# Grouped attention layer: where the query and value evacuations stand in the softmax rounds

## The reference, cut to what matters

```python
q = hidden_state @ Wq + bq
k = encoder_hidden_state @ Wk + bk
v = encoder_hidden_state @ Wv + bv
q = q.reshape(b, l, KVH, GROUPS, HD).transpose(0, 2, 3, 1, 4)
...
scores = jnp.einsum('bkgld,bksd->bkgls', q, k) * scale
scores = scores + encoder_attention_mask[:, :, None, :, :]
attn = jax.nn.softmax(scores, axis=-1)
out = jnp.einsum('bkgls,bksd->bkgld', attn, v)
out = out.transpose(0, 3, 1, 2, 4).reshape(b, l, H)
out = out @ Wo + bo
x = out + hidden_state
...
return (x - mu) * jax.lax.rsqrt(var + EPS) * gamma + beta
```

## Time and profile before

| what | value |
|---|---|
| median of 3 runs | 2687.87 us (2686.5 to 2689.95) |
| profiled execution | 2687.89 us, its span 2686.1 us |
| busy, share of the span | PE 2477.0 us, 92%; DVE 1280.0 us, 48%; ACT 1089.2 us, 41%; POOL 1106.1 us, 41% |
| chain that ended last | PE 79%, DVE 8%, ACT 6%, POOL 3%, issue 3% |
| grouped layer | about 810 to 1200 us of the span |

### The profile page before, as it was taken

One profiled execution on the slowest core, in us unless ns is written; L12 is line 12 of the kernel. 1 busy time (PEld: TensorE's weight loads), 2 busy tenths in 40 slices (PEclk: granted clock), 3 DMA queues, 4 the chain that ended last, 5 costly groups with the idle time before them and its releaser, 6 DMA issues.

```text
span 2686.1 us, 47930 instructions
## 1 busy us (share of the span) xinstructions
PE 2477.0 (92%) x18464; PEld 2080.4 (77%) x18464; DVE 1280.0 (48%) x2527; ACT 1089.2 (41%) x3705; POOL 1106.1 (41%) x1972
## 2 busy tenths in 40 slices
PE   7999998999997788758889899999899999899999
PEld 5887886888886666647778788888788888688887
DVE  4555564323226878764555533322355555432322
ACT  4555553111117777754565511111355555311111
POOL 2454446400035888873454571003335444640000
PEclk9999999999998989878999999999999999999999
DMA  4112213111122222221232241102211211311100
GB/s 154 56 56 74 86 48 95 59 47 48 57 71 72 82 91 70 74 67 45 94 111 77 82 129 48 47 23 69 87 48 49 84 53 48 95 59 48 47 32 16
DMA packets 110320, 181.25 MB, mean 67 GB/s; under 512 B 7888, under 2 KB 43408, under 8 KB 109072
## 3 DMA queue, kind: packets, MB, share of 16 engines
q1 hardware_dynamic: 110096, 178.19, 20.2%
HBM read 132.02 MB, written 46.14 MB: 66 GB/s over the span
## 4 chain that ended last, share of the span: by engine, by line
PE 79%; DVE 8%; ACT 6%; POOL 3%; issue 3%; DMA 1%; SPq 0%; DVEq 0%; POOLq 0%; ACTq 0%
PE banks L317 70%; PE banks L453 4%; ACT plain_high L697 4%; PE banks L480 3%; DVE neg_max L948 2%; DVE plain_high L944 2%; POOL plain_high L1268 1%; DVE plain_work L953 1%; PE banks L504 1%; DVE rounded_work L1046 1%; DVE rounded_work L1020 1%; DVE stats L1072 1%; POOL rounded_high L308 0%; PE banks L442 0%; ACT plain_high L684 0%
## 5 line engine op out<-in xcount | busy, mean ns | idle before, releaser
L317 PE MATMUL banks<-rounded_work,rounded_low 128*128 128x512 f32 (+1 forms) x2688 | 534.7, 357 | 58.4 <-issue 35.2
L1268 POOL TENSOR_SCALAR plain_high<-plain_high,inv_sum 128x128 f32<-128x128 f32 (+1 forms) x1024 | 389.6, 403 | 410.2 <-DVE inv_sum L966 409.7
L317 PEld LDWEIGHTS banks<-rounded_work,rounded_low 128*128 128x128 f32 x2688 | 446.7, 200 | 125.6 <-issue 53.7
L317 PE MATMUL banks<-rounded_work,rounded_high 128*128 128x512 f32 (+1 forms) x2400 | 485.4, 356 | 8.4 <-DMA rounded_work<-ctx_split 5.8
L925 ACT ACTIVATE plain_work<-banks,columns 128x512 f32<-128x512 f32 x192 | 132.5, 690 | 865.3 <-PE banks L317 865.3
L317 PEld LDWEIGHTS banks<-rounded_work,rounded_high 128*128 128x128 f32 x2400 | 397.1, 191 | 75.8 <-issue 10.0
L1244 DVE CAST rounded_work<-plain_work 128x512 fp32r<-128x512 f32 x192 | 99.3, 517 | 694.1 <-ACT plain_work L925 682.9
L317 PE MATMUL banks<-rounded_low,rounded_work 128*128 128x512 f32 x1728 | 413.1, 391 | 0.0
L317 PE MATMUL banks<-rounded_high,rounded_work 128*128 128x512 f32 (+1 forms) x1728 | 392.7, 380 | 0.0
L317 PEld LDWEIGHTS banks<-rounded_low,rounded_work 128*128 128x128 f32 x1728 | 322.3, 188 | 68.8 <-issue 3.0
L317 PEld LDWEIGHTS banks<-rounded_high,rounded_work 128*128 128x128 f32 x1728 | 311.8, 190 | 60.4 <-issue 1.4
(11 more groups left out here) (101 smaller groups left out, 3055.3 us busy)
## 6 DMA issues: line engine op xcount, KB each, us to landing
plain_work<-x SPq DMA_DIRECT2D x96, 256.0 KB, 2.8
plain_work<-mlp_w SPq DMA_DIRECT2D x96, 256.0 KB, 2.7
rounded_work<-ctx_split SPq DMA_DIRECT2D x24, 1024.0 KB, 5.9
u<-plain_work SPq DMA_DIRECT2D x48, 256.0 KB, 3.1
plain_work<-u SPq DMA_DIRECT2D x12, 1024.0 KB, 7.2
x<-plain_work SPq DMA_DIRECT2D x48, 256.0 KB, 2.1
plain_work<-attention_w SPq DMA_DIRECT2D x44, 256.0 KB, 2.7
plain_work<-inputs_t SPq DMA_DIRECT2D x8, 1024.0 KB, 8.0
```

What stands on the lines that cost most here:

```text
L317: mm = pe.matmul(dst, lhs(i), rhs(j), start=first and n == 0, stop=last and n == 2, skip_group_check=True)
L1268: last = pool.tensor_scalar(part, part, inv_sum[:, R % 2, r, g:g + 1], 1.0, ALU.mult, ALU.mult)
```

## The change

In act_gqa the evacuation of the next pair's first queries moves from behind round 2's last exponential to between those of banks 1 and 2, and the evacuation of the next pair's values moves likewise in round 3. In dve_gqa the low part of the queries moves from behind the inversions and dve_again to ahead of the inversions. Counts and shapes of the instructions are the same, and PE, POOL and SP have the same order as before.

```diff
@@ act_gqa
                 act_heads(act, y, p, 0)
                 if more:
                     act_keys(act, y, p + 1, 0)
-                act_round(act, y, p, 2, (p, 1), nothing)
-                if more:
-                    act_queries(act, y, p + 1, 0)
+
+                def queries():
+                    if more:
+                        act_queries(act, y, p + 1, 0)
+
+                def values():
+                    if more:
+                        act_values(act, y, p + 1, 0)
+
+                act_round(act, y, p, 2, (p, 1), queries)
                 act_heads(act, y, p, 1)
-                act_round(act, y, p, 3, (p, 2), nothing)
-                if more:
-                    act_values(act, y, p + 1, 0)
+                act_round(act, y, p, 3, (p, 2), values)
                 act_heads(act, y, p, 2)
@@ dve_gqa
                 if more:
                     dve_keys(dve, y, p + 1, 0)
-                dve_round(dve, y, p, 2, (p, 1), nothing)
+
+                def queries():
+                    if more:
+                        dve_queries(dve, y, p + 1, 0)
+
+                dve_round(dve, y, p, 2, (p, 1), queries)
                 if p:
                     dve_again(dve, y, 2 * p - 1)
-                if more:
-                    dve_queries(dve, y, p + 1, 0)
                 dve_heads(dve, y, p, 1)
```

## The result

| | kernel before | changed kernel |
|---|---|---|
| median (range, runs) | 2687.49 us (2684.92 to 2689.95, 12) | 2695.91 us (2692.7 to 2703.1, 12) |
| ratio, 95% interval | 1 | 1.0035 (1.0027 to 1.0044) |
| profiled execution, its span | 2687.89 us, 2686.1 us | 2694.08 us, 2692.3 us |

A forecast was written before the change was run, and what follows sets the result against it. No engine is full; a pair is a ring of waits between engines. First pair 1.97, two pairs 0.85 each, four 0.07 each and slow value blocks 4.98 sum to 8.93 us on 2687.87: 2696.8 us, range 2694 to 2700.

The forecast's parts named there:

- Queries on ScalarE and VectorE, -0.07 us: Round 2: second inversion 0.71 us later, but the queries' low part (0.78 us) no longer behind it; net -0.07 us.
- GpSimd, +0.78: Round 2: the low part delays the first inversion, so GpSimd's normalisation starts and ends 0.78 us later.
- The values' end, and the wait on ScalarE: Round 3, fifth pair: value matmuls end at 1041.21; ScalarE, there at 1040.47, waits with eight exponentials queued behind.
- 0.7 us and more in each of seven pairs: Sign: ScalarE's idle ahead of line 744, ended by the value matmuls, is at least this long in every pair.
- above 3 us where the block is slow: Sign: that same ScalarE idle exceeds 3 us where the value matmuls run at 1.2 GHz.
- Pair lengths: Round 2 to next round 0: about 21.2 us, or 23.7 with a slow value block, instead of 20.33 and 21.11.
- VectorE's wait for ScalarE's heads: Sign: VectorE's wait at L993, L998 in the changed program, grows.
- no wait for TensorE ahead of the mask addition: Sign: VectorE's wait for TensorE ahead of the next mask addition is gone.
- The value block's clock: Gaps ahead of the values widen from 0.75 to about 1.5 us; two of six further blocks run slow, 4.98 us.
- the rival of 2706.8 us: All value blocks run at 1.2 GHz, 18.9 us more in sum; chance 0.12.
- POOL has caught up by then.: GpSimd's 0.78 us delay is absorbed by 1.61 us idle ahead of the next pair's round 0 normalisation.
- Outside the grouped layer: Sign: times there stay unchanged; more than 2 us of difference there means the reasoning missed something.

The follow-up runs named there:

- queries_only: The changed kernel with the values' evacuation put back behind round 3's exponentials, the queries still moved; 2691.32 us, ratio 1.0018.
- values_only: The changed kernel with the queries put back on ScalarE and VectorE, only the values' evacuation still moved; 2689.59 us, ratio 1.0012.
- again_middle: The kernel before with dve_again moved between the two inversions of rounds 1 and 2; 2694.13 us, ratio 1.0015.
- after_gap_fill: The changed kernel with two extra matmuls of ones ahead of each bank's transposes in rounds 2 and 3; 2691.22 us, ratio 1.0004.
- after_all_fill: after_gap_fill with also 10, 3 and 2 extra matmuls ahead of the attention matmuls of rounds 1, 2 and 3; 2687.85 us, ratio 0.9993.
- before_all_fill: The kernel before with the same extra matmuls as after_all_fill; 2680.59 us, ratio 0.9976.

## Why the prediction was right, step by step

- *Queries on ScalarE and VectorE, -0.07 us.* Right. The second inversion still waits for ScalarE, 1.56 us, and in queries_only, without the values, the stretch is 20.27 us against 20.33.
- *GpSimd, +0.78.* Right to the hundredth (7.55 us behind the start, and 7.55 or 7.56 in every pair from the second to the seventh).
- *The values' end, and the wait on ScalarE.* Right: the forecast gave 1041.21 - 1040.47 = 0.74 us, measured 0.75; values_only shows that it shrinks to 0.36 without GpSimd's part. Of the signs named, "0.7 us and more in each of seven pairs" failed in the third and seventh pair (0.22 and 0.24 us, where a slow query block came ahead), and "above 3 us where the block is slow" in the fourth (2.18 us).
- *Pair lengths.* Forecast 21.18 us, measured 21.13 and 21.14 in the second, fifth and sixth pair; 21.39 in the third and seventh, where a query block at 4.3 us came ahead. First pair: forecast 24.02 (22.05 + 1.97), measured 23.97.
- *VectorE's wait for ScalarE's heads.* Wrong in sign: it was to grow, and fell from 0.96 to 0.23 us. The wait moved to the second inversion of round 3, which stands ahead of the heads and waits for the last exponential: 2.80 us, where it had waited 1.63. The other half of that sign, no wait for TensorE ahead of the mask addition, came true (0.29 us before).
- *The value block's clock.* Right in kind, too high in number for this execution: one more slow block, the fourth pair's, which cost 1.98 us, where 2 x 2.49 were put. What was to bring it about was read wrong: the last gap ahead of the values did not widen "to about 1.5 us", it stayed at 0.76 us; the change turns one gap in the fifth pair into four. The third, fourth, fifth and seventh pair of the changed kernel all have these four gaps (0.28 or 0.29 us, then three of 0.76), and only the fourth's value block is slow. Nothing in the forecast told which, so two of six was a guess, and one came. The Trainium skill (TensorE: Matmul & The Clock Gate, section "A second HAM failure mode: psum-queue depth-cycling") says that short idle times between groups of matmuls make the clock swing. The runs with filled gaps agree: no value block is slow in them, and the ratios are 1.0004 and 0.9993 against 1.0035. Not every block is hit, as the rival of 2706.8 us would have had it.
- *"POOL has caught up by then."* This step was wrong, twice. It was read from the 1.61 us of idle in the fourth pair; the pair that the forecast walks has none there, and the delay is still 0.73 us at that place (7.50 against 6.77). And between round 2's normalisation and that idle lie round 3's transposes, which wait for GpSimd. Missing from the sum is a term for the output projection behind them: 2.35 us in the sixth pair's stretch of the profiled run (1.29 net, since the third pair's output projection was no longer slow), 5.9 us in queries_only. So the forecast put 8.93 us into the stretches of the change, where 6.30 were measured, and nothing into the others, where 1.29 were. These two errors partly cancel, and that the total came out near is in part luck.
- *Outside the grouped layer.* The forecast named 2 us as the bound. The layer began 2.07 us sooner. Among the profiles shown here it began anywhere from 807.39 to 811.12 us behind the same instructions, so this is the scatter of the part ahead, and a reason why 6.2 us between two profiles and 8.4 us between two medians are no contradiction.

What stays open is which block loses its clock in a given execution. In the changed kernel the third and the fourth pair have the same history (a query block of 4.33 and 4.39 us, then three gaps of 0.76 us ahead of the values), and the value blocks take 2.87 and 4.84 us; its runs spread over 10 us against 5 before. With one profiled execution of each kernel I can't say how many blocks are slow in the typical one.

## What to carry to other kernels

An evacuation that waits for a later result, put into the middle of a queue, makes everything behind it wait: before moving it forward, compare the time at which its input is ready with the time at which the queue gets there, and add every delay that the same change puts ahead of that input. An engine's idle time at the end of a loop does not show that it has caught up; look at who waits for it before that idle. Where matmul groups stand apart by fractions of a microsecond, hold the clock first (cheap matmuls in the gaps) and compare the orders after that, since otherwise a shorter chain can come out slower.

## What the runs showed of the hardware that I had not expected

- 24 matmuls of 128 columns take 2.87 us at 2.4 GHz and 5.36 us at 1.2 GHz (granted clock 0.50 from 892.94 to 898.30 in again_middle). No idle time among the transposes ahead of that slow block is longer than 0.77 us; but blocks at full clock have the same ahead of them (943.77 in the changed kernel, 2.87 us). A gap filled with two matmuls of ones leaves idle times of 0.30 us, and all value blocks of after_gap_fill and after_all_fill took 2.87 or 2.88 us.
- Added work made both kernels faster: by ratios of 0.0042 (after_all_fill against the changed kernel) and 0.0024 (before_all_fill). TensorE's busy time rose from 2479.1 to 2507.2 us and from 2477.0 to 2504.0 us for that.
- A slow clock hides gaps: in the kernel before, round 3's transposes at 1.2 GHz (16 in 3.08 and 3.51 us, fourth and fifth pair) kept TensorE busy until GpSimd was ready, and the projection behind them ran at 2.4 GHz (3.01 us). Made early and fast, as in queries_only, the same transposes stood apart, and the projection was the slow one (3.62 us and more in four of the first five pairs). Not each time: in the changed kernel's sixth pair they stood apart, and the projection took 2.99 us.
